# Layer 1's quantised y turned and its scales spread by DMA, the last down tiles by ScalarE and POOL, one block's middle tap added by TensorE, affine rows first, new orders

## The reference: what is computed

```
layer 0, per sequence b (language l = itok_B_0_8[b]):
  h = relu(x @ W1[l] + b1[l]);  z = layernorm(x + h @ W2[l] + b2[l]) * gamma[l] + beta[l]
  x = x + bitlinear(gelu(bitlinear(z, 256 -> 1024)), 1024 -> 256)
layer 1, per sequence b (subject s = itok_B_0_7[b]):
  y = x @ W[s].T + b[s]                       # 256 -> 256
  u = bitlinear(y, 256 -> 1024)
  c[t] = tap0 * u[t-1] + tap1 * u[t] + tap2 * u[t+1] + convb   # per channel, along tokens
  x = x + bitlinear(silu(c), 1024 -> 256)
```

## Time and profile before

| | us |
|---|---|
| median of 3 runs | 305.05 (302.7 to 305.88) |
| the profiled execution, its own time | 302.91 |
| its span in the trace | 300.4 |
| ACT, DVE, POOL, PE busy | 247.5, 255.3, 265.7, 268.8 |
| granted clock of PE, tenths, first five of 40 slices | 9, 7, 7, 7, 9, then 9 throughout (full) |

### The profile page before, as it was taken

The page is one execution under the profiler, slowest core; times in us unless marked ns, Lnnn a source line. Parts: engine busy times, 40 slices in busy tenths (PEclk is TensorE's granted clock), DMA queues, the critical chain, the costliest instruction groups (busy, mean ns, idle before and its releaser), DMA issues.

```text
span 300.4 us, 6735 instructions
## 1 busy us (share of the span) xinstructions
PE 268.8 (89%) x1854; PEld 194.0 (65%) x1854; DVE 255.3 (85%) x625; ACT 247.5 (82%) x416; POOL 265.7 (88%) x390
## 2 busy tenths in 40 slices
PE   7698789999989999999998998989989999866794
PEld 7575446566666566666656676767767677635693
DVE  0379899989897999678899999999999999999681
ACT  1759999989899889487769969979799897979752
POOL 2398989889899799999998989999999999999972
PEclk9777999999999999999999999999999999999998
DMA  5896856676675332661122314233394232343575
GB/s 177 304 354 194 275 150 150 157 137 163 158 197 87 72 84 59 130 149 31 24 59 71 70 37 104 40 71 85 29 175 116 53 89 79 100 105 72 136 190 183
DMA packets 87047, 36.92 MB, mean 123 GB/s; under 512 B 71334, under 2 KB 84442, under 8 KB 87011
## 3 DMA queue, kind: packets, MB, share of 16 engines
q1 hardware_dynamic: 80560, 28.40, 40.4%
q10 hardware_dynamic: 6450, 8.10, 8.4%
HBM read 16.04 MB, written 4.19 MB: 67 GB/s over the span
## 4 chain that ended last, share of the span: by engine, by line
PE 42%; ACT 17%; issue 17%; POOL 12%; DVE 4%; DMA 4%; SPq 3%; ACTq 1%; POOLq 0%; DVEq 0%
PE banks L1401 8%; PE banks L1343 5%; PE banks L1362 5%; PE banks L1481 5%; PE banks L1437 4%; PE banks L1458 4%; POOL raw_all L893 3%; DMA raw_all<-in_w2a 3%; ACT ry L619 3%; PE banks L1344 2%; PE banks L1379 2%; ACT g L656 2%; POOL mid L886 2%; POOL r L832 2%; ACT g L592 2%
## 5 line engine op out<-in xcount | busy, mean ns | idle before, releaser
L893 POOL TENSOR_TENSOR raw_all<-raw_all,mid 128x1024 f32<-128x1024 f32 x32 | 63.6, 1996 | 0.0
L645 ACT ACTIVATE banks<-apad,taps 128x512 f32<-128x512 f32 x64 | 44.2, 703 | 15.6 <-DVE apad L1113 15.6
L886 POOL TENSOR_SCALAR mid<-apad,taps,convb 128x512 f32<-128x512 f32 x64 | 48.7, 768 | 0.0
L1120 DVE SCALAR_TENSOR_TENSOR raw_all<-apad,taps,banks 128x512 f32<-128x512 f32 x64 | 46.0, 738 | 1.2 <-ACT banks L645 1.1
L1064 DVE TENSOR_REDUCE am<-g 128x1 f32<-128x1024 f32 x32 | 38.8, 1214 | 7.5 <-ACT g L592 7.2
L1113 DVE TENSOR_TENSOR apad<-banks,dqb 128x512 f32<-128x512 f32 x64 | 43.0, 684 | 2.2 <-PE banks L1437 1.6
L592 ACT ACTIVATE g<-banks,dqz 128x1024 f32<-128x1024 f32 x32 | 35.6, 1117 | 6.9 <-PE banks L1344 4.8
L1343 PE MATMUL banks<-tern,qT 128*128 128x512 bf16 x128 | 38.1, 379 | 2.7 <-ACT qcT L584 2.7
L832 POOL TENSOR_SCALAR r<-g,qs 128x1024 uint16<-128x1024 f32 x32 | 35.8, 1118 | 2.9 <-DVE qs L1076 2.6
L1437 PE MATMUL banks<-yT,tern 128*128 128x512 bf16 x128 | 35.4, 379 | 2.7 <-DVE raw_all L1120 2.5
L1458 PE MATMUL banks<-id,raw_all 128*128 128x128 f32 x256 | 33.6, 275 | 4.6 <-ACT g L656 4.3
(11 more groups left out here) (139 smaller groups left out, 599.3 us busy)
## 6 DMA issues: line engine op xcount, KB each, us to landing
out_y<-xs SPq DMA_DIRECT2D x32, 128.0 KB, 2.0
xs<-in_x ACTq DMA_DIRECT2D x7, 512.0 KB, 4.2
x2T<-in_xT ACTq DMA_DIRECT2D x4, 512.0 KB, 5.1
wl<-in_cwl SPq DMA_DIRECT2D x8, 256.0 KB, 2.8
xT<-in_xT ACTq DMA_DIRECT2D x3, 512.0 KB, 4.3
cw<-in_cw SPq DMA_DIRECT2D x16, 64.0 KB, 2.9
raw_all<-in_w1a SPq DMA_DIRECT2D x1, 1024.0 KB, 5.0
raw_all<-in_w2a SPq DMA_DIRECT2D x1, 1024.0 KB, 9.8
```

What stands on the lines that cost most here:

```text
L645: act.activation(bank(BANK_U[g % 3]), apad[:, f, 2:S + 2], ACT.Copy, scale=taps[:, f, 2:3]).then_inc(p_last, 1)
L886: pool.tensor_scalar(mid[f // 2 % 2][:, f % 2, :], apad[:, f, 1:S + 1], taps[:, f, 1:2], convb[:, f:f + 1], ALU.mult, ALU.add).then_inc(p_ ...
L893: pool.tensor_tensor(c[:, 2 * q:2 * q + 2, :], c[:, 2 * q:2 * q + 2, :], mid[q % 2][:, :, :], ALU.add).then_inc(p_sum, 1)
L1120: dve.scalar_tensor_tensor(out=conv[b % 2][:, f, :], in0=apad[:, f, 0:S], scalar=taps[:, f, 0:1], in1=bank(BANK_U[(KH * b + f) % 3]), op0= ...
```

## The change

Sizes: `ry` is now uint16 (integer plus 128), `ryT` and `down2_out` are new in SBUF, `dqy_rows` is a new tensor in the chip's main memory, `mid_last` a new buffer for the last block's middle tap.

- **y by DMA.** `round_y` writes uint16; SP's `transpose_y` is one DMA transpose of 128 by 1024 values; `lead_q` reads its result in SBUF. PE's eight transposes are gone.
- **Scales by DMA.** SP's `store_scales` writes `dqy` to main memory as a row of 512, `load_scales` reads it back to all 128 partitions of `dqb`. PE's four transposes and ACT's copy are gone.
- **Down tiles.** Tiles 0 and 2 also go by `dequant2` and `add2`, except in the last sequence, where all four go by DVE's `final2`. `add2` and `scale_of_down` work on a pair of tiles at once; `store2` stores a pair, 256 KB.
- **Middle tap of block 7.** `tap_sum` handles blocks 0 to 6 (its last call one block only). Block 7's middle tap stays in `mid_last`, and `transpose_conv` adds it in PSUM with a second transpose per tile.
- **Affine first.** SP issues `langs`, `gamma`, `beta` ahead of the adapter's loads; PE's `affine_columns` and `affine_rows(0)` stand ahead of `adapter_out(0, 0)`. `up1(0, 0)` no longer waits for the second weight's scale.
- **New orders** in all lists of all engines.

```diff
+            def transpose_y(b):
+                sp.wait_ge(p_ry[0], b + 1)
+                sp.wait_ge(p_ry[1], b + 1)
+                wait(sp, p_yTe, b)
+                sp.dma_start_transpose(ryT[:, :, :, :].rearrange("p k j c -> p (k j) c"),
+                                       ry[:, :, :].rearrange("p k d -> p (k d)")).then_inc(p_yT, 16)
+            def store_scales(b):
+                sp.wait_ge(p_dqy, b + 1)
+                sp.dma_start(dqy_rows[b].rearrange("(k p) -> p k", p=P), dqy[:, :], allow_slow_non_contiguous=True).then_inc(p_row, 16)
+            def load_scales(b):
+                sp.wait_ge(p_row, 16 * (b + 1))
...
+                wait(sp, p_a, KH * (b - 1))
+                sp.dma_start(dqb[b % 2][:, :], dqy_rows[bass.ds(b, 1), :].to_broadcast([P, S])).then_inc(p_dqb[b % 2], 16)
 SP slot2(s):
+                once(s, B - 4, transpose2, 3, 2)
+                once(s, B - 4, transpose2, 3, 3)
+                on(store2, s - 5, 1)
+                on(store2, s - 4, 0)
+                on(store_scales, s + 2)
+                on(transpose_y, s + 2)
+                on(load_scales, s + 2)
                 on(transpose2, s, 0)
                 on(transpose2, s, 1)
...
 ACT slot2(s):
+                on(silu, s - 2, 0)
+                on(round2, s - 3, 3)
                 on(last_tap, s - 1, 3)
                 on(last_tap, s - 1, 4)
                 on(silu, s - 2, 1)
                 on(round_y, s, 0)
                 on(round_y, s, 1)
+                on(dequant2, s - 3, 1)
+                on(last_tap, s - 1, 5)
+                on(round2, s - 2, 0)
                 on(last_tap, s - 1, 6)
-                on(lead_scales, s)
+                on(dequant2, s - 3, 2)
                 on(silu, s - 2, 2)
                 on(lead_q, s)
...
 POOL:
             def tap_sum(b, q):
+                n = min(2, TURNED - 2 * q)
...
+                pool.tensor_tensor(c[:, 2 * q:2 * q + n, :], c[:, 2 * q:2 * q + n, :],
+                                   mid[q % 2][:, 0:n, :], ALU.add).then_inc(p_sum, 1)
+            def add2(b, p):
+                pool.wait_ge(p_part[p], 2 * b + 2)
+                n = PAIR * b + p
+                pool.tensor_tensor(xs[:, n, :, :], xs[:, n, :, :], down2_out[:, 2 * p:2 * p + 2, :], ALU.add) \
+                    .then_inc(p_o[p], 1)
 PE transpose_conv(b, k):
+                for f in range(TURNED, KH):
+                    block = bank(bank_c(b, k) + f // KT)[:, (f % KT) * P:(f % KT + 1) * P]
+                    pe.matmul(block, conv[b % 2][:, f, k * P:(k + 1) * P], id32[:, :], start=True, stop=False,
+                              is_transpose=True)
+                    ins = pe.matmul(block, mid_last[b % 2][:, k * P:(k + 1) * P], id32[:, :], start=False,
+                                    stop=True, is_transpose=True)
 PE up1(b, j):
-                    pe.wait_ge(s_wsc, 4)
+                    if j > 0:
+                        pe.wait_ge(s_wsc, 4)
 endings (DVE; ACT; POOL):
-                untranspose_wide(2); final2(7, 2); untranspose_wide(3)
+                final2(7, 1); final2(7, 2); untranspose_wide(3); final2(7, 3)
-                round_wide(2); untranspose_wide(2); round_wide(3); dequant2(7, 1); untranspose_wide(3); dequant2(7, 3)
+                round_wide(2); dequant2(6, 3); untranspose_wide(2); round_wide(3); untranspose_wide(3)
+                round2(7, 0); round2(7, 1); round_wide(2); add2(6, 0); scale_of_down(7, 0); add2(6, 1)
+                scale_of_down(7, 1); round_wide(3)
```

More of the change, by code:

```diff
@@ L242, in build_program @@
         dqy = sb("dqy", [P, TB])
-        ry = sb("ry", [P, TB, D])
-        yT = [sb(f"yT{k}", [P, KD, S], BF16) for k in range(2)]
+        ry = sb("ry", [P, TB, D], U16)
+        ryT = sb("ryT", [P, TB, KD, P], U16)
+        yT = [sb(f"yT{k}", [P, TB, KD, P], BF16) for k in range(2)]
+        dqy_rows = nc.dram_tensor("dqy_rows", [B, S], F32, kind="Internal").ap()
+        mid_last = [sb(f"mid_last{k}", [P, S]) for k in range(2)]
+        TURNED = KH - 1
         apad = sb("apad", [P, KH, SP2])
@@ L446, in load_ids @@
+                once(s, B - 2, transpose2, 6, 3)
             def load_ids():
@@ L468, in first @@
[L468 to L472, removed]
@@ new lines, in first @@
+                lead_q(0); gelu(7, 1); lead(1, 0); gelu(7, 2); last_tap(0, 0); last_tap(0, 1); lead(1, 1)
+                last_tap(0, 2); last_tap(0, 3); round_y(1, 0); last_tap(0, 4); round_y(1, 1); last_tap(0, 5)
+                lead(2, 0); gelu(7, 3); dequant_down1(6, 0); last_tap(0, 6); lead(2, 1); lead_q(1)
+                dequant_down1(6, 1); last_tap(0, 7); last_tap(1, 0); last_tap(1, 1); last_tap(1, 2); silu(0, 0)
+                round_y(2, 0); round_y(2, 1); last_tap(1, 3); lead(3, 0); silu(0, 1); last_tap(1, 4); round2(0, 0)
@@ L884, in middle_tap @@
                     pool.wait_ge(s_wsum, 4)
-                wait(pool, p_sum, TB * b + f // 2 - 1)
-                pool.tensor_scalar(mid[f // 2 % 2][:, f % 2, :], apad[:, f, 1:S + 1], taps[:, f, 1:2],
+                if f < TURNED:
+                    wait(pool, p_sum, TB * b + f // 2 - 1)
+                    out = mid[f // 2 % 2][:, f % 2, :]
+                else:
+                    wait(pool, p_cT[TB - 1], b - 1)
+                    out = mid_last[b % 2][:, :]
+                pool.tensor_scalar(out, apad[:, f, 1:S + 1], taps[:, f, 1:2],
                                    convb[:, f:f + 1], ALU.mult, ALU.add).then_inc(p_mid, 1)
@@ new lines, in first @@
+                scale2(0, 0); final1(7, 0); first_tap(1, 3); dequant(1, 4); dequant(1, 5); inverse2(0, 0)
+                dequant(1, 6); first_tap(1, 4); absmax2(0, 1); final1(7, 1); scale2(0, 1); absmax2(0, 2)
+                inverse2(0, 1); scale2(0, 2); first_tap(1, 5); first_tap(1, 6); absmax_y(3, 0); dequant(1, 7)
+                absmax2(0, 3); inverse2(0, 2); absmax_y(3, 1); scale_y(3); scale2(0, 3); first_tap(1, 7)
+                inverse2(0, 3); inverse_y(3); dequant(2, 0); dequant(2, 1); dequant(2, 2); first_tap(2, 0)
```

558 lines of the change are left out of this document (255 added, 303 removed).

## The result

The changed kernel takes **342.15 us** (median of 4 runs, 339.62 to 346.63) against 303.88 for the kernel before on the same chip: ratio 1.123, 95% interval 1.110 to 1.135. I had forecast 295. Its profiled execution took 340.96 us, with a span of 339.2.

A forecast was written before the change was run, and what follows sets the result against it. It took the ring of waits PE → DVE → ACT, DVE fullest, to bound the second layer, and PE layer 1. Slots −4.0, tail −2.0, crossing −1.5, head −1.5, reordering 0 gave −9.0: 295 us, range 289.5 to 302.5.

The forecast's parts named there:

- X: Second layer: time of the scales' store until their load can be issued, taken as 3.1 us, bad end 7.6.
- the scales come late: Rival: dequant waits for dqb, costing from X = 5.3, slower than before at 6.3; 310 us, chance 0.08.
- 12.2 + X: Second-layer loop from dequant through the scales' store and load to the next block's dequant: 15.3 us at X = 3.1.
- Covered, slack 1.0: y's DMA transpose lands 2.9 us after round_y, hidden by 3.9 us of ACT work before lead_q.
- Reordering of layer 1 otherwise: First layer's new orders: no work removed, PE near full, so 0 us, bounds ±1.5.
- The period, 17.5: Second layer in steady state: 17.5 us per block, 1.0 less than 18.50, bounds 17.2 and 18.5.
- The terms on POOL: Second layer, per block: one-block tap_sum 1.1 us, 128×512 add 1.27, POOL's work from 17.5 to 17.2.
- POOL stays in the way: Rival: late inputs to POOL keep the second layer's period at 18.2 or above; about 301 us, chance 0.17.
- The sum: Whole kernel: steady slots, tail, crossing, head and layer-1 reordering total −9.0 us.
- Four periods: Second layer, round_y of blocks 3 to 7: four periods × 1.0 = −4.0 us, bounds 0 and −5.2.
- Head and crossing: Head: earlier affine work and first round_z, −1.5 us; crossing, y of blocks 0 to 2: PE work removed, −1.5.
- Tail: After 256.5 us: less POOL work, last tile leaving by DVE, later stores; −2.0 us, bounds −0.5 and −3.

The follow-up runs named there:

- e11: e8 with the scales stored to HBM as four transfers of 128 pieces of 4 bytes, in place of 128 pieces of 16 bytes: 337.39 us.
- e10: e8 plus four transfers that scatter the same scales in 4-byte pieces into SBUF, where nothing uses them: 302.84 us.
- e2: The changed kernel with y's transpose issued ahead of the store of the scales in SP's order: 376.71 us.
- e1: The changed kernel with the scales stored as 128 pieces of 16 bytes instead of 512 of 4, so in a wrong order: 304.38 us.
- e5: e1 with DVE's dequant reading the scales at a stride of 16 bytes, which restores the needed order: 323.35 us.
- e6: e5 with four loads of the first layer put back to about their distances before the change: 317.62 us.
- e8: e6 with the plain read: the changed kernel with 16-byte pieces and first-layer loads apart, scales in a wrong order: 300.22 us.
- b3: The kernel before with the affine vectors loaded and used first and PE's first up1 not waiting for the second weight's scale: 304.59 us.
- e9: e8 with scales in the needed order: PE turns them, ACT copies them, SP stores four rows behind y's transpose: 305.43 us.
- e12: e9 with a block's first code transpose issued ahead of the scales' load: 304.64 us.

## Why the prediction was wrong

**The step that failed is X, the store of the scales**: "I take 3.1, and 7.6 as the bad end". It was 7.9 to 10.9. The nearest rows were small *loads*; nothing showed a small write to HBM, and e11 and e10 show that this is what counts. The bad end should have been no end. A late store stood in the rival "the scales come late", at a chance of 0.08, and its deciding point, 6.3, was passed. But its place was wrong: `dequant` waits for `dqb` 2.8 us in all, while ACT waits 29.0 for y's transpose. Its loop, 12.2 + X, gives 20.1 to 23.1 us; the four periods were 20.3, 25.5, 22.5 and 25.4, 23.4 on average, so the loop doesn't contain the path that sets them. Only e2, where y's transpose goes first, takes the rival's path.

The Trainium skill (DMA: Bandwidth & Descriptors, Specifications) says that transfers under 512 B make the DMA engine read, modify and write. No run here shows that step itself. The 9.5 us at 4 bytes would fit it, but pieces of 16 bytes are under 512 too and landed in 2.0, and pieces of 4 bytes into SBUF in 2.2, so the size of 512 isn't what divided slow from quick here.

**"Covered, slack 1.0"** for y's transpose failed by the same cause, and this is the wait that set the blocks: 2.8 us of landing became up to 9.3 beside the store, on a slack of 1.0. I had priced the store alone, not what is in flight with it. e1 shows the step right otherwise: landing 3.1, no wait.

**"Reordering of layer 1 otherwise: 0, bounds ±1.5"** failed: 5.7 us between e5 and e6. I counted instructions, not the distances of the 512 KB loads; the hole came from four loads in another place.

**The period, 17.5**, was nearly right once the store is mended: of the eight periods of e1 and e8 six are 17.5 or 17.6 us, one is 18.6 and one 19.4. The terms on POOL were right; the changed kernel's groups, 183 to 300 us:

```profile
L934 POOL TENSOR_TENSOR xs<-xs,down_out 128x512 f32<-128x512 f32 x9 | 11.4, 1268 | 0.0
L915 POOL TENSOR_TENSOR raw_all<-raw_all,mid 128x512 f32<-128x512 f32 x6 | 6.5, 1090 | 0.0
```

1.27 and 1.1 were the prices. In e8 POOL is still busy 54.46 of 55.5 us. Whether it binds there, as the rival "POOL stays in the way" had it, no run shows.

**The sum**, read from e8 against the profile before: −2.8 of span for −9.0. So even without the two large losses it was three times too hopeful. Four periods −2.1 for −4.0 (−3.8 if the long one had been 17.6). Head and crossing: block 3's `round_y` is 1.3 earlier, for −3.0. The head start isn't kept: the first `round_z` moved as I said (22.89 in the changed kernel for 25.68), but the first `gelu` starts at 31.57 for 32.13, and in e8 the last one isn't earlier at all, 147.78 for 147.72. b3 finds 0.2%, within its interval, in the head's part. Tail +0.6 for −2.0: DVE does end the last tile, as intended, but PE and DVE now wait for each other between the last tiles. DVE in e8:

```profile
292.84 0.48 DVE L1166 SCALAR_TENSOR_TENSOR xs<-banks,dq,xs 128x256 f32<-128x256 f32 x1 [1.14 <-PE banks L1488]
...
294.46 0.48 DVE L1166 SCALAR_TENSOR_TENSOR xs<-banks,dq,xs 128x256 f32<-128x256 f32 x1 [0.81 <-PE banks L1488]
```

That last reading is argued, not shown; no kernel undid the tail alone. e11 has a slow store with the loads apart, and at 337.39 it is 4.8 below the changed kernel (one run, another session), near the 4.2 and 5.7 above.

## What to carry to other kernels

Price a transfer by a row with the same direction, memory and size of piece; where there is none, give the cost no upper end, and ask what else is in flight when it is slow. Before turning engine work into a small round trip through HBM, look at the size of its pieces: here 4 bytes were dear and 16 were not. Count also what it takes to have the data in the needed order: each way tried here from larger pieces gave the gain back (e5, e9, e12). An order of instructions is also an order of loads: compare the times of the large issues before and after.

## What was unexpected of the hardware

- 512 writes of 4 bytes to HBM land after 9.5 us, 256 of 8 bytes after 3.4, 128 of 16 bytes after 2.0, and 4 × 128 pieces of 4 bytes into SBUF after 2.2. In the packet records of the changed kernel the 512 packets of a store all start within 1.0 us: what is late is the completion. The same holds for y's transpose behind it: in the block of 242.06 its 1024 packets of 256 bytes have all started by 244.64, but `lead_q` starts at 248.51.
- y's transpose, issued while such a store is open, completes about when the store does, from the same queue (up to 9.3 us against 3.1) and from another (9.3).
- An fp32 stride of 16 bytes in one operand of a DVE `tensor_tensor` raised 128x512 from 684 to 1111 ns.
- Code transposes of 128x1024 land in 2.7 us, in 9.85 under five 512 KB loads.
